# DLRM tower on one Trainium2 core: one gram piece per tile behind the ninth lookup unit, layer 3 in four column groups, second gathers without a wait

## The reference, cut to what matters

```python
# 2048 records, 26 tables of rows of 128 floats; 10 of the 26 have 1000 rows
e = stack([tbl_f[ids[:, f]] for f in range(26)], axis=1)          # (2048, 26, 128)
all_vecs = concatenate([dense[:, None, :], e], axis=1)            # (2048, 27, 128)
inter = einsum('bnd,bmd->bnm', all_vecs, all_vecs)                # gram of each record
h = concatenate([dense, inter[:, upper triangle, 351 pairs], dense], axis=1)
h = maximum(h @ W_top1 + b_top1, 0)      # 607 -> 512, "layer 1"
h = maximum(h @ W_top2 + b_top2, 0)      # 512 -> 256, "layer 2"
y = h @ W_top3                           # 256 -> 1,   "layer 3"
```

## Time and profile before

| | |
|---|---|
| median of 3 runs | 370.9 us (370.31 to 371.07) |
| the profiled execution | 370.56 us |
| its span in the profile | 368.6 us |
| PE busy | 338.4 us, 92% |
| POOL busy | 245.3 us, 67% |
| DVE busy | 241.6 us, 66% |
| ACT busy | 140.9 us, 38% |
| mean granted clock of PE | 0.995 |

### The profile page before, as it was taken

One profiled execution on the slowest core, in us unless ns is written; L12 is line 12 of the kernel. 1 busy time (PEld: TensorE's weight loads), 2 busy tenths in 40 slices (PEclk: granted clock), 3 DMA queues, 4 the chain that ended last, 5 costly groups with the idle time before them and its releaser, 6 DMA issues.

```text
span 368.6 us, 14267 instructions
## 1 busy us (share of the span) xinstructions
PE 338.4 (92%) x6096; PEld 309.5 (84%) x6096; DVE 241.6 (66%) x702; ACT 140.9 (38%) x232; POOL 245.3 (67%) x260
## 2 busy tenths in 40 slices
PE   0686689999999999999999999999999999999797
PEld 0585589999899898989899998989999998998675
DVE  4999999998565856578565974677664884601300
ACT  2246432535143541344343441444442450447132
POOL 5777777777777777777777777777767777760000
PEclk9989999999999999999999999999999999999999
DMA  6999944332244212611243111521244112220000
GB/s 192 284 245 245 290 140 124 79 106 54 58 152 123 59 50 67 205 56 52 55 145 125 50 51 50 188 83 50 52 140 129 50 50 55 73 57 4 18 2 0
DMA packets 16567, 36.90 MB, mean 100 GB/s; under 512 B 5462, under 2 KB 8542, under 8 KB 16544
## 3 DMA queue, kind: packets, MB, share of 16 engines
q1 hardware_dynamic: 8335, 19.77, 18.0%
q0 software_dynamic: 8192, 16.79, 17.6%
q10 hardware_dynamic: 16, 0.01, 0.0%
HBM read 36.54 MB, written 0.01 MB: 99 GB/s over the span
## 4 chain that ended last, share of the span: by engine, by line
PE 85%; DVE 7%; issue 3%; DMA 3%; POOL 2%; ACT 0%; DVEq 0%
PE hid L387 14%; PE gram L413 13%; PE look_ps L341 8%; PE vec_act L314 7%; PE look_ps L343 7%; PE look_odd L341 7%; PE look_odd L343 7%; PE hid L394 7%; DVE onehot L557 5%; PE hid L341 4%; PE hid L343 4%; DMA vecs<-tbl,ids_sb 2%; DVE look_lo L565 2%; POOL vecs L297 2%; PE small L356 1%
## 5 line engine op out<-in xcount | busy, mean ns | idle before, releaser
L297 POOL DMA_INDIRECT vecs<-tbl,ids_sb x256 | 245.1, 957 | 85.1 <-issue 75.9
L557 DVE TENSOR_SCALAR onehot<-step_ids,row_no 125x256 fp32r<-125x256 int32 x640 | 199.0, 381 | 74.6 <-PE look_odd L343 35.0
L532 ACT COPY vecs_T<-vec_act 128x512 f32<-128x512 f32 x64 | 46.3, 732 | 102.2 <-PE vec_act L314 102.2
L341 PE MATMUL look_odd<-onehot,look_hi 125*128 125x256 f32 x256 | 67.3, 300 | 4.6 <-DVE look_lo L565 4.6
L341 PE MATMUL look_ps<-onehot,look_hi 125*128 125x256 f32 x256 | 67.8, 301 | 2.3 <-DVE look_lo L565 2.3
L343 PE MATMUL look_ps<-onehot,look_lo 125*128 125x256 f32 x256 | 63.7, 284 | 0.0
L343 PE MATMUL look_odd<-onehot,look_lo 125*128 125x256 f32 x256 | 62.9, 283 | 0.0
L413 PE MATMUL gram<-vecs_T 128*27 128x26 f32 x4096 | 52.8, 192 | 5.9 <-issue 3.3
L413 PEld LDWEIGHTS gram<-vecs_T 128*27 128x27 f32 x4096 | 44.1, 104 | 15.0 <-issue 9.1
L341 PEld LDWEIGHTS look_odd<-onehot,look_hi 125*128 125x128 f32 x256 | 48.8, 191 | 5.5 <-DVE look_lo L565 5.2
L341 PEld LDWEIGHTS look_ps<-onehot,look_hi 125*128 125x128 f32 x256 | 49.2, 192 | 3.2 <-DVE look_lo L565 2.7
(11 more groups left out here) (70 smaller groups left out, 282.2 us busy)
## 6 DMA issues: line engine op xcount, KB each, us to landing
step_ids<-look_ids SPq DMA_DIRECT2D x15, 640.0 KB, 4.5
raw<-tbl SPq DMA_DIRECT2D x10, 448.0 KB
vecs<-tbl,ids_sb POOLq DMA_INDIRECT x256
dense_new<-dense SPq DMA_DIRECT2D x8, 128.0 KB
dense_T<-dense SPq DMA_DIRECT2D x8, 128.0 KB, 2.9
raw<-tbl SPq DMA_DIRECT2D x10, 52.0 KB
step_ids<-look_ids SPq DMA_DIRECT2D x1, 512.0 KB
w_sb<-w SPq DMA_DIRECT2D x1, 512.0 KB
```

The costliest lines, as they stand in the source:

```text
L297: nc.gpsimd.indirect_dma_start(out=vecs[j][:, k, :], out_offset=None, in_=tables[k], in_offset=bass.IndirectOffsetOnAxis(ap=ids_sb[:, t, k ...
L341: nc.tensor.matmul(bank, look_hi[:, f, ch, :], onehot[:, i % SLOTS, c, :], start=ch == 0, stop=False)
L532: return engine_copy(vecs_T[j][:, :, lo:lo + GROUP], bank[:, :, :].rearrange("d v b -> d b v"))
L557: last = nc.vector.tensor_scalar(onehot[:, i % SLOTS, c, :], step_ids[a][0:LOOK_K, f - a * LOOKUPS // 2, :], row_no[0:LOOK_K, ch:ch + 1], ...
```

## The change

PE: the two halves of the gram become one piece, `gram_all`, behind unit 8 (the ninth), and in the odd tiles layer 3 follows it; unit 9 comes last. Layer 3 becomes eight matmuls of 64 columns, whose outputs stand at partitions 0, 32, 64 and 96 (its weights are padded from one column to 32, 31 of them zeros), and the output is written as 4 rows of 64 a pair. POOL: the wait at the ninth gather of a tile goes. Behind the loop, gram 14 comes first, then `pairs_out`, layer 1's first half, all four turn groups of tile 15, layer 1's second half and gram 15; ACT's order follows, and DVE gets one more wait, for its own last fold.

```diff
@@ gather
-                        if k == HALF_GATHERS and t >= 2:
-                            pool.wait_ge(gram_half0, t - 1)
-                            pool.sem_inc(gather_begun, 1)
@@ layer 3
+                def layer3_parts(bank):
+
+                    for c in range(H2 // P):
+                        for g in range(Y_PARTS):
+                            last = nc.tensor.matmul(bank[g * QUAD:(g + 1) * QUAD, :], w3_sb[:, c, :],
+                                                    h2_T[:, c, g * PAIR // Y_PARTS:(g + 1) * PAIR // Y_PARTS],
+                                                    start=c == 0, stop=c == H2 // P - 1)
+                    return last
...
-                    for c in range(H2 // P):
-                        last = nc.tensor.matmul(bank, w3_sb[:, c:c + 1], h2_T[:, c, :],
-                                                start=c == 0, stop=c == H2 // P - 1)
-                    last.then_inc(y_ready, 1)
+                    layer3_parts(bank).then_inc(y_ready, 1)
@@ gram
-                def gram_first(t, j, pair):
+                def gram_all(t, j, pair):
 
                     wait_for_vecs(t, j, pair)
-                    gram_part(j, 0).then_inc(gram_half0, 1)
+                    gram_part(j, 0)
                     gram_part(j, 1)
-
-                def gram_second(j):
                     gram_part(j, 2).then_inc(gram_half1, 1)
                     gram_part(j, 3).then_inc(gram_ready, 1)
@@ tile on PE
                     unit(4)
-                    gram_first(t, j, pair)
                     if mlp and j == 1:
                         layer2(pair - 1)
                     unit(5)
...
                     unit(8)
-                    unit(9)
-                    gram_second(j)
+                    gram_all(t, j, pair)
                     if mlp and j == 1:
                         layer3(pair - 1)
+                    unit(9)
@@ behind the loop on PE
-                tile(last - 1, 0, pairs - 1, look=False)
+                gram_all(last - 1, 0, pairs - 1)
+                pairs_out(last - 2, 0, pairs - 1)
+                layer1(pairs - 2, 0, look=False)
+                turn_half(last, 1, pairs - 1, 0)
+                turn_half(last, 1, pairs - 1, 1)
                 layer1(pairs - 2, 1)
-                gram_first(last, 1, pairs - 1)
-                gram_second(1)
+                gram_all(last, 1, pairs - 1)
@@ result on ACT
-                    nc.scalar.copy(y_row, bank).then_inc(y_copied, 1)
+                    nc.scalar.copy(y_rows, bank).then_inc(y_copied, 1)
                     act.wait_ge(y_copied, m + 2)
-                    act.dma_start(out[:, bass.ds(m * PAIR, PAIR)], y_row).then_inc(y_out, 16)
+                    act.dma_start(out[bass.ds(m * Y_PARTS, Y_PARTS), :], y_rows[0:P:QUAD, :]).then_inc(y_out, 16)
```

More of the change, by code:

```diff
@@ L58 @@
 QUAD = 32
+Y_PARTS = P // QUAD
 PAIRS = VECS * (VECS - 1) // 2
@@ L133, in build @@
         h2_T = raw[0][:, 0:H2 // P * PAIR].rearrange("p (c b) -> p c b", c=H2 // P)
-        y_row = raw[1][0:1, 0:PAIR]
+        y_rows = raw[1][:, 0:PAIR // Y_PARTS]
         w1_sb = sb("w1_sb", [P, 1 + CHUNKS, H1])
@@ L138, in build @@
         b2_sb = sb("b2_sb", [P, H2 // P])
-        w3_sb = sb("w3_sb", [P, H2 // P])
+        w3_sb = sb("w3_sb", [P, H2 // P, QUAD])
         ident = sb("ident", [P, P])
@@ L153, in build @@
         hid2 = hid1
-        y_ps = small[0:1, 0:PAIR]
+        y_ps = small[:, 0:PAIR // Y_PARTS]
         pairs_end = look_bank[:, 0:CHUNKS * P].rearrange("p (c b) -> p c b", c=CHUNKS)
@@ L160, in build @@
         hid2_end = [small[:, 0:PAIR], vec_banks[1][:, 0:PAIR]]
-        y_ends = [hid1[0:1, 0, :], look_odd[0:1, 0:PAIR]]
+        y_ends = [hid1[:, 0, 0:PAIR // Y_PARTS], look_odd[:, 0:PAIR // Y_PARTS]]
         def raw_table(f):
@@ L181, in build @@
         gather_begun, fold_begun = sem("gather_begun"), sem("fold_begun")
-        gram_half0, gram_half1 = sem("gram_half0"), sem("gram_half1")
+        gram_half1 = sem("gram_half1")
         ident_in, weights_in, mask_in, row_no_in = sem("ident_in"), sem("weights_in"), sem("mask_in"), sem("row_no_in")
@@ L266, in _ @@
                 load_weight(b2_sb[:, :], b2)
-                load_weight(w3_sb[:, :], w3)
+                load_weight(w3_sb[:, :, :].rearrange("p c n -> p (c n)"), w3)
                 load_weight(w1_sb[0:CHUNK, 1:3, :], w1_pairs[0:2 * CHUNK, :].rearrange("(c k) n -> k c n", k=CHUNK))
@@ L524, in _ @@
                 pe.wait_ge(h2_copied, pairs + 2)
-                for c in range(H2 // P):
-                    end = nc.tensor.matmul(y_ends[1], w3_sb[:, c:c + 1], h2_T[:, c, :], start=c == 0, stop=c == H2 // P - 1)
-                end.then_inc(y_ready, 1)
+                layer3_parts(y_ends[1]).then_inc(y_ready, 1)
             def copy_group(engine_copy, bank, j, q):
@@ L611, in _ @@
                 turn(last - 2)
+                dve.wait_ge(folded, last - 1)
                 turn(last - 1)
@@ L757, in _ @@
                 last = tiles - 1
-                tile(last - 1, 0, pairs - 1, look=False)
+                copy_pairs(last - 2, 1)
+                merge(1, pairs - 1, True)
+                merge(1, pairs - 1, False)
+                place_dense(last, 1, pairs - 1)
+                relu1(pairs - 2, 0)
+                for q in range(GROUPS):
+                    copy(last, 1, q)
                 relu1(pairs - 2, 1)
@@ L796 @@
         "b2": np.ascontiguousarray(np.asarray(inputs["b_top2"]).reshape(H2 // P, P).T),
-        "w3": np.ascontiguousarray(np.asarray(inputs["W_top3"]).reshape(H2 // P, P).T),
+        "w3": np.ascontiguousarray(np.pad(np.asarray(inputs["W_top3"]).reshape(H2 // P, P).T[:, :, None],
+                                          ((0, 0), (0, 0), (0, QUAD - 1))).reshape(P, -1)),
         "fold_mask": np.ascontiguousarray(np.broadcast_to(
@@ L808 @@
           for name, a in arrays.items()}
-    out = nc.dram_tensor("y", (1, dense.shape[1]), F32, kind="ExternalOutput").ap()
+    out = nc.dram_tensor("y", (dense.shape[1] * Y_PARTS // (2 * P), 2 * P // Y_PARTS), F32, kind="ExternalOutput").ap()
     build(nc, ap["dense"], ap["ids"], ap["look_ids"], [ap[f"tbl_{f}"] for f in large],
```

2 lines of the change are left out of this document (1 added, 1 removed).

## The result

The changed kernel takes 382.96 us (median of 4 runs, 381.29 to 384.86), the one before 370.99 us on the same chip: a ratio of 1.0325, 95% interval 1.0272 to 1.0379. The forecast was 372.4 us with a range to 376.5. The sign was right, the size was not: 12 us slower where 1.5 were expected. The profiled execution took 381.29 us, its span is 379.3.

What follows compares the result with a forecast made beforehand. PE's own row of work was taken as the bound, POOL close behind. The terms -4.2 - 4.5 + 5.2 + 1.0 + 2.1 + 0.6 + 1.6 = +1.8 on the profiled 370.56 us gave 372.4 us, range 366.0 to 376.5.

Steps and rivals of the forecast that it cites:

- 1, 2: breaks and layer 3: PE: one gram break of 0.30 us less in tiles 0 to 13, -4.2; layer 3's column groups overlap, -4.5 us.
- 3: late fold: PE waits 0.75 us at pairs_out for DVE's fold, in tile 1 and six even loop tiles: +5.2 us.
- 4: gathers beside grams: Running gathers slow PE's grams; whole grams take 2.8 to 3.8 us: +1.0 us, bounds -5 to +4.
- 5: stops in tiles 0 to 3: Whole grams in first-run code stop for instruction fetch; 0.7 us each in tiles 1 to 3, tile 0 unchanged: +2.1 us.
- 5: stop in tile 15: Tile 15's one-piece gram in first-run code already stops for 2.13 us; the sum had no term for it.
- 6: order behind the loop: Behind the loop PE idles 1.1 us before gram 14, transposes meet ACT's copies, less some savings: +0.6 us.
- 6: stop in tile 14: Tile 14's whole gram, undisturbed in first-run code, stops for instruction fetch, 0 to 2.13 us: +1.6 us.
- Column groups don't overlap: Layer 3's four column groups on PE save nothing: 376.9 us, chance 0.10.
- fetch hidden: Instruction fetch causes no new stops in grams, so 3.7 us of cost goes: 368.7 us, chance 0.15.
- the fold is in time: DVE is ready 0.75 us sooner, so pairs_out does not wait for the fold: 367.2 us, chance 0.12.
- the loop outgrows what is held: 24 more instructions cause fetches in every loop pass, ten more stalls of 0.7 us: 379 us, chance 0.04.
- POOL's idle time falls under the grams: POOL's idle time lies under PE's grams, so gathers disturb them less, -5 instead of +1: 366.4 us, chance 0.13.

Runs made afterwards that it cites:

- combo: Changed kernel with grams of tiles 0, 1 and 14 in halves, the old order behind the loop, and the fold ahead of unit 4: 368.01 us, 0.9905.
- b_layer3: Kernel before with layer 3 in four column groups and nothing else changed: 369.11 us, ratio 0.9926.
- a_nogather: Changed kernel with the gathers of tiles 2 to 15 left out: 368.98 us, ratio 0.9930.
- b_pad128: Kernel before with 128 already fulfilled waits in place of one at the start of PE's program: 371.58 us, ratio 1.0002.
- old_tail: Changed kernel with the order behind the loop as before and tile 14's gram in halves: 376.33 us, ratio 1.0129.
- b_no_ninth: Kernel before without POOL's wait at the ninth gather and nothing else changed: 372.52 us, ratio 1.0029.
- b_nogather: Kernel before with the gathers of tiles 2 to 15 left out: 356.05 us, ratio 0.9579.
- combo_pad128: combo with 128 already fulfilled waits in place of one at the start of PE's program: 369.87 us, ratio 0.9943.

## Why the prediction was wrong in size

| part | predicted | measured |
|---|---|---|
| 1, 2: breaks and layer 3 | -8.7 | about -8.9 |
| 3: late fold | +5.2 | +6.7 |
| 4: gathers beside grams | +1.0 | about 0 |
| 5: stops in tiles 0 to 3 | +2.1 | +5.8 |
| 5: stop in tile 15 | kept | -2.3 |
| a stop in layer 2 behind gram 15 | none | +0.7 |
| 6: order behind the loop | +0.6 | about +1.8 |
| 6: stop in tile 14 | +1.6 | +2.4 |
| lower clock | none | +4.6 |
| sum | +1.8 | about +10.8 |

The profiled span grew by 10.7, the median by 12.0; the last 1.3 are not in the table, which is of one execution. From the start of the turns behind the loop (332.06; in the changed kernel from the start of gram 14's wait, 337.85) to gram 15 it is 12.55 us before and 19.91 after; of the difference the stop is 2.4, the clock 3.2, and the 1.8 that is left is the order.

**Breaks and layer 3** held. Without gathers a pass of combo is 1.34 us shorter; two breaks of 0.30 and layer 3's 0.59 make 1.19, so the break, if anything, is worth 0.37 (the table takes 0.30). Layer 3 went to 0.37 where "an overlap of 2.5" gave 0.40; with the 8.7 ns a record of part 1 in place of 9.3 the overlap is 2.8 and the estimate 0.35. What I did not see is that its gain in the loop hangs on unit 9 standing behind it (b_layer3).

**The late fold** is the first step that was mis-sized, "3.65" against "2.9". PE's side was right: with no wait `pairs_out` would have started at 256.30, 2.91 behind unit 9's last matmul. DVE's was short: its unit is 1.36 us long (1.28 to the start of the fold, 253.71 to 254.99) and not 1.14. The one of the earlier trace rows was a fast one: the median unit is 1.32 us long in the kernel before, and 1.14 where the gathers are left out. And I ended the sum at the fold's end, 257.21, when PE began at 257.45. These 0.24 us from DVE's end to PE's start come on top. Together 1.15 instead of 0.75, six times and not seven. Removing it gave back 5.6 by the medians and 7.6 by the ratios; in the passes it was half of the wait.

**The fetch stops** had the right mechanism and the wrong size, "0 to 1.16 each, I take 0.7". I took tile 0's stop as unchanged ("has its stall already"). It was the stop of a half gram (1.34 from start to start); in the whole gram it was 3.30, 2.0 more, and tiles 1 to 3 had 1.27 on average. The bound that fits is the one I had in the earlier trace rows for a whole gram, 2.13: a_nogather shows 2.2 to 2.4 in each. What a break bought was time: with lookups between two halves PE mostly needs longer for 256 instructions than the 3.3 to 3.5 us of section 3, in one gram of 512 it does not. Tile 15's stop I carried over as fixed, and it vanished: b_pad128 shows that such a stop is set by where the gram lies in the code, which the change moves. The stop in layer 2 behind it (0.92 us between two starts that are else 0.22 apart) was in no term. The Trainium skill (Runtime: NRT & Kernel Launch, Instruction fetch mechanics) calls the crossing of a block mostly hidden. By these runs that holds for lookups, with few instructions in a microsecond, and for the loop once it is held (no packet of instructions between 134 and 336 us); a gram is dense enough that it stands for up to 3.3 us.

**The lower clock** was missing from the sum altogether, and it is the step that failed outright: my own sum held idle times of PE in a row behind the loop, and their effect on the clock was not asked for. Behind the loop 1.36 us of waiting for copies and a stop of 2.41 came close together, and from 344.2 on, 0.9 us behind the stop's end, stood 6.9 us at the 1.2 GHz level (the 0.57 ahead of layer 1 falls inside it and did not bring it on). The stop of 2.13 us in tile 15's gram had not done that in the kernel before. I priced each idle time by its own length, and together they cost 3.2 more. old_tail, where wait and stop are gone, has no fall: the same matmuls take 1.30 instead of 2.56.

**Gathers beside the gram**, the part with the widest bounds, came out near zero: they cost 16 us before (4.2% by the ratios) and 15 in the changed kernel (3.9%), a difference within its noise of some 3 us; by the distances, stops aside, they add 13.6 us to the grams of tiles 0 to 13 before and 14.0 in the changed kernel. Part 4 put today's cost at 11 to 12, from busy times; by distances it is 13.6.

Two small slips in the working change nothing: the first stop of the weight loads in the earlier trace rows begins at 97.37 and not 97.28, and 32 gathers at 1.24 to 1.25 us are 39.7 to 40.0.

**The rivals.** "Column groups don't overlap", "fetch hidden", "the fold is in time" and "the loop outgrows what is held" are all excluded: 0.37 us, stops, six waits, and 18 packets as before, of which none lies in the later passes. So is "POOL's idle time falls under the grams", with part 4 near 0 and not at -5. The range failed because it was made of rivals that each turn one term off, and no case had several terms at their bad ends at once with one term missing.

## What to carry to other kernels

Before joining pieces of a dense instruction stream, look at what the breaks hide: here breaks of 0.3 us and the old order also kept the code's fetch, the fold and the clock out of sight. Join them where the code is already held (the loop's later passes) and leave the first-run code ahead of and behind the loop split: that version gains 0.95%. And price a stop of PE with what follows it: if windows show the clock halved behind such a stop, its real cost is its length plus half of that stretch.

## What was not expected of the hardware

- The granted clock went to 0.51 behind 3.3 us of stop in the gram of tile 0 and behind idle times of 1.36 and 2.41 us; the stretch was 3.4 us long in the first case, 6.9 in the second. It is no fixed price: the stop of 2.32 us in tile 15's gram is followed by no fall in the kernel before, the same stop (2.49 and 2.02 us) by 3.4 us at about half clock in b_no_ninth and b_nogather, and so are those of 2.37 us in b_pad128 and combo_pad128; combo has such a stretch behind the 1.55 us of tile 2.
- A stop in the gram moves with code that does no work: 128 fulfilled waits at the start, 64 instructions more, took away 1.3 us in tile 0 and moved tile 15's stop by 96 matmuls, with no change of the total (1.0002). The places are 256 instructions apart, and a stop ends 2.2 to 2.9 us behind the start of a packet of instructions.
- Taking out all gathers behind the second tile makes the kernel 4.2% faster, and by the distances between starts nearly all of that lies in the grams (49.5 to 34.5 us); PE's lookups, turns and layers up to the last pass keep their length.
- Behind the short layer 3 in a loop's last place the next pass's first matmul starts 0.65 us behind layer 3's last, and 0.19 where no jump follows.
